# A GNN layer on one core: weights, bias and last nodes loaded by the Activation engine's queue

## The chip, the cores and the metric

One core of a Trainium2 chip runs the kernel. The metric is the device time of one execution in microseconds (us), lower being better. The kernel before was timed three times.

## The reference

With x of shape [5000, 64], a dense adjacency matrix adj of shape [5000, 5000] and everything in float32:

```python
h = jnp.maximum(_layernorm(x, axis=-1), 0.0)
neighbors = (adj @ h) / (num_neighbors[:, None] + 1e-7)
out = jnp.concatenate([h, neighbors], axis=-1) @ fc_w.T + fc_b   # fc_w is [64, 128]
return x + jax.nn.relu(out)
```

adj is 100 MB, everything else together under 3 MB.

## The kernel before, in words

The kernel uses that adj @ h @ W equals adj @ (h @ W). It first forms g = h @ W_neighbor for all nodes (64 columns), keeps it in SBUF as `g_sb`, and then multiplies adjacency tiles by it. So adj is read once, and every tile of it is used by TensorE as soon as g of its 128 source nodes is there.

**Loads of adj.** The host lays adj out transposed, in six groups of columns. A load (`LOADS`) is up to four row tiles of a group: in group 0 a load is 4 x 2560 floats for each of 128 lanes, one run of 40 KB a lane, 5,242,880 bytes. All 33 loads are issued by SP (line 259) in order into the buffer `raw`. In group 0 three loads fit in it. The fourth and later ones wait for `load_used`, which TensorE raises when it has multiplied the load whose place is taken (lines 255 to 256, 633 to 634). `landed` says that a load has arrived.

**Preparation.** The 40 row tiles of x are normalized in five sets of eight, b = 0 to 4. DVE and ACT compute the layer norm of a set (`normalize`, lines 407 to 436, `ln_square`, `ln_std`), TensorE transposes it (`turn`, line 579), ACT copies it to `ht` (line 357), TensorE multiplies it by the weights `w_both` (`weigh`, lines 582 to 598), and ACT copies the neighbour part to `g_sb` (line 363) while DVE adds the bias to the node's own part (`add_bias`, line 448). Set 0 comes before the first adjacency tile, sets 1 to 4 are put between tiles (`TURN_AFTER`, `WEIGH_AFTER`). Sets 0 to 3 need only the two main loads of x (`load_x`, semaphore `x_loaded[0]`). Set 4 also needs the last 392 nodes (`x_loaded[1]`), loaded in two pieces: lanes 0 to 95 (98,304 bytes) and lanes 96 and 97 (2 KB), the second only after DVE has cleared what pads them.

**Small loads.** The weights `fc_t` are loaded twice into `w_both`, in each load 64 lanes with two runs of 256 bytes, after DVE has cleared `w_both` (`weights_cleared`). The bias is one run of 256 bytes. A matrix product of ones and the bias row (line 683) spreads it over all lanes, and DVE copies it (`bias_copied`). It uses an accumulator that group 1 needs later. The 5000 neighbour counts `nn` are loaded by ACT (lines 331 and 333) after set 1 is transposed, the last 8 rows of adj by GpSimd (lines 294 to 299).

**Order on the queues before.** SP issues `load_x(0)`, `load_x(1)`, the 96 lanes of the last nodes (line 268), waits for `weights_cleared`, issues the weights twice (line 272), then adj. ACT runs one Sqrt first, which brings its table in (line 373), then issues the bias (line 325) and the two lanes (line 327). TensorE waits for the bias first, spreads it, then `turn(0)`, waits for the weights, `weigh(0)`, and starts on the loads.

Of the kernel before, what the change touches and what calls it, by code (L numbers as in the profile page):

```python
# [44 lines left out]
def gnn_layer(nc, x, adj_groups, num_neighbors, fc_t, fc_b, out):  # L45
# [9 lines left out]
    N, F = x.shape  # L55
# [11 lines left out]
    PAD0 = LAST_LANES // 32 * 32  # L67
# [56 lines left out]
    with ExitStack() as ctx:  # L124
# [8 lines left out]
        x_sb = sb("x_sb", [LANES, TILES, F])  # L133
# [13 lines left out]
        w_both = sb("w_both", [2 * F, 2, 2 * F])  # L147
# [65 lines left out]
        def tail(v):  # L213

            return v[0:LAST_LANES, ROWS:TILES, :].rearrange("p t f -> p (t f)")

        def tail_nodes(v):
            return v[TAIL0:N, :].rearrange("(p t) f -> p (t f)", t=RUN)
# [32 lines left out]
        def sync_program(sp):  # L251
            def load(n):
                g, m, i0, i1 = LOADS[n]
                w = WIDTH[g]
                if loads_before(n):
                    sp.wait_ge(load_used, loads_before(n))
                r = RUN if m < FULL else TAIL_RUN
                rows = adj_groups[g][m * BLOCK:m * BLOCK + r * LANES, 0:w].rearrange("(p i) c -> p (i c)", i=r)
                sp.dma_start(raw[:, place(n):place_end(n)], rows[:, i0 * w:i1 * w]).then_inc(loaded(n)[0], 16)

            def load_x(k):
                r = slice(ROWS // 2 * k, ROWS // 2 * (k + 1))
                sp.dma_start(x_sb[:, r, :], x[0:TAIL0, :].rearrange("(p r) f -> p r f", r=ROWS)[:, r, :]  # L263
                             ).then_inc(x_loaded[0], 16)

            load_x(0)
            load_x(1)
            sp.dma_start(tail(x_sb)[0:PAD0], tail_nodes(x)[0:PAD0]).then_inc(x_loaded[1], 16)  # L268
            sp.wait_ge(weights_cleared, 1)
            for s in range(2):  # L270
                k = slice(s * F, (s + 1) * F)
                sp.dma_start(w_both[k, s, :].rearrange("r (k c) -> r k c", k=2), fc_t.rearrange("(k r) c -> r k c", k=2)  # L272
                             ).then_inc(weights_loaded, 16)
            for n in range(len(LOADS)):
                load(n)

            sp.wait_ge(out_ready, LAST)
            sp.dma_start(out[0:TAIL0, :].rearrange("(p r) f -> p (r f)", r=ROWS), flat(out_sb[:, 0:ROWS, :])
                         ).then_inc(stored, 16)
            sp.wait_ge(stored, 16)  # L280
# [40 lines left out]
        def scalar_program(act):  # L321
            def load_few():

                act.wait_ge(bias_cleared, 1)
                act.dma_start(bias_row[0:1, :], fc_b.rearrange("(a f) -> a f", a=1)).then_inc(bias_loaded, 16)
                act.wait_ge(x_cleared, 1)
                act.dma_start(tail(x_sb)[PAD0:LAST_LANES], tail_nodes(x)[PAD0:LAST_LANES]).then_inc(x_loaded[1], 16)

            def load_counts():
                act.wait_ge(nn_cleared, 1)  # L330
                act.dma_start(nn[:, 0:ROWS], num_neighbors[0:TAIL0].rearrange("(p r) -> p r", r=ROWS)
                              ).then_inc(nn_loaded, 16)
                act.dma_start(nn[0:LAST_LANES, ROWS:TILES],
                              num_neighbors[TAIL0:N].rearrange("(p t) -> p t", t=RUN)).then_inc(nn_loaded, 16)

            def ln_square(b):
                act.wait_ge(ln_dve, LN_OPS * b + 3)
                nc.scalar.activation(sums[0][:], cen[:], ACT.Square).then_inc(ln_act, 1)  # L338

            def ln_std(b):  # L340
                act.wait_ge(ln_dve, LN_OPS * b + 5)
                nc.scalar.activation(std[:], var[:], ACT.Sqrt).then_inc(ln_act, 1)

            def copy_turned(b):
                act.wait_ge(turned_done, b + 1)
                if b >= 2:
                    act.wait_ge(weighed, b - 1)
                if b == SETS - 1:
                    act.wait_ge(rem_cleared, 2)

                    k = turned[HALF:LANES, :].rearrange("k (t p) -> k p t", t=RUN)[:, 0:LAST_LANES, :]
                    nc.scalar.activation(ht_rows[HALF:LANES, :].rearrange("k (p t) -> k p t", t=RUN), k, ACT.Copy)

                    nc.scalar.activation(
                        ht_rem[HALF:LANES, 0:REM * REM_STEP].rearrange("k (p t z) -> k p t z", t=RUN, z=REM_STEP)[:, :, :, 0],
                        k[:, LAST_LANES - REM // RUN:LAST_LANES, :], ACT.Copy)
                nc.scalar.activation(ht[b % 2][:], turned[:], ACT.Copy).then_inc(turned_copied, 1)  # L357

            def copy_g(b):
                act.wait_ge(weighed, b + 1)  # L360
                to = g_sb[:, BT * b:BT * (b + 1), :].rearrange("p (s i) f -> p i s f", s=2)
                for k in range(2):
                    nc.scalar.activation(to[:, 2 * k:2 * k + 2, :, :], weighed_parts(k, 1), ACT.Copy).then_inc(g_copied, 1)  # L363

            def copy_spread(b):
                act.wait_ge(spread_done, b + 1)
                w = BLOCK if b != ALONE else BLOCK // 2 + SIDE
                nc.scalar.activation(rnn_bc[:, b, 0:w], y[b % 2][:, 0:w], ACT.Copy).then_inc(spread_copied, 1)  # L368


            act.wait_ge(warm_ready, 1)
            nc.scalar.activation(std[:, 0:1], warm[:], ACT.Sqrt)
            load_few()
            for b in range(SETS):
                ln_square(b)
                ln_std(b)
                if b == 0:
                    copy_turned(0)
                else:
                    copy_g(b - 1)  # L380
                    copy_turned(b)
                if b == 1:
                    load_counts()
            copy_g(SETS - 1)
            for b in range(SETS):
                copy_spread(b)
            act.wait_ge(out_ready, LAST + 1)
            act.dma_start(tail_nodes(out), tail(out_sb)).then_inc(last_stored, 16)
            act.wait_ge(last_stored, 16)

        def vector_program(dve):
            nc.vector.memset(warm[:], 1.0).then_inc(warm_ready, 1)
            nc.vector.memset(x_sb[PAD0:LANES, ROWS:TILES, :], 0.0).then_inc(x_cleared, 1)
            nc.vector.memset(w_both[:], 0.0).then_inc(weights_cleared, 1)
            nc.vector.memset(nn[:], 1.0).then_inc(nn_cleared, 1)

            def parts(b):
# [174 lines left out]
        def tensor_program(pe):  # L572
            def turn(b):
                pe.wait_ge(ln_dve, LN_OPS * (b + 1))
                if b:
                    pe.wait_ge(turned_copied, b)
                for i in range(RUN):
                    c = slice(i * LANES, (i + 1) * LANES)
                    last = nc.tensor.transpose(turned[:, c], h_pairs[b % 2][:, c], ident[:])  # L579
                last.then_inc(turned_done, 1)  # L580

            def weigh(b):

                pe.wait_ge(turned_copied, b + 1)
                if b:
                    pe.wait_ge(self_copied, 2 * b)
                apart = b == SETS - 1
                w = 3 * F if apart else 4 * F
                for i in range(RUN):
                    c = i * LANES  # L590
                    last = nc.tensor.matmul(weighed_tiles(i)[:, 0:w], ht[b % 2][:, c:c + LANES], flat(w_both[:])[:, 0:w],  # L591
                                            start=True, stop=True)
                    if apart:

                        h = ht_rows[F:LANES, i:REM0 - TAIL0:TAIL_RUN] if i < TAIL_RUN else ht_rem[F:LANES, :]
                        last = nc.tensor.matmul(weighed_tiles(i)[:, w:4 * F], h, w_both[F:LANES, 1, F:2 * F],  # L596
                                                start=True, stop=True)
                last.then_inc(weighed, 1)
# [75 lines left out]
            def flip_last():  # L674
                for i in range(2):
                    pe.wait_ge(scaled, LAST + i + 1)
                    nc.tensor.transpose(acc[i][0:LAST_LANES, 0:2 * F], sums[0][:, i * LAST_LANES:(i + 1) * LAST_LANES],  # L677
                                        ident[:]).then_inc(flipped, 1)


            pe.wait_ge(bias_loaded, 16)
            pe.wait_ge(bias_cleared, 2)
            nc.tensor.matmul(acc[SETS - 1][:, 0:F], ones[:], bias_row[:], start=True, stop=True).then_inc(bias_spread, 1)  # L683
            pe.wait_ge(ident_ready, 1)
            turn(0)
            pe.wait_ge(weights_loaded, 32)
            weigh(0)
            for n in range(len(LOADS)):
                g, m, i0, i1 = LOADS[n]
                pe.wait_ge(*loaded(n))  # L690
# [55 lines left out]
```

## Time and profile before

| What | Value |
|---|---|
| median of 3 runs | 246.09 us (246.04 to 246.28) |
| the profiled execution | 245.87 us, its span 244.4 us |
| TensorE busy | 209.6 us, 86% of the span |
| VectorE, ScalarE, GpSimd busy | 41.6, 15.1, 6.1 us |
| DMA | 102.79 MB, mean 421 GB/s |
| mean granted TensorE clock | 0.965 |

The span goes from the first instruction to the last. The profiled execution took 1.5 us more than its span, and was 0.22 us below the median. Times within the span are counted from its start. In the slice table each digit is the busy share, in tenths, of one fortieth of the span, 6.1 us. PE is TensorE, DVE VectorE, ACT ScalarE, POOL GpSimd, SP SyncE. A name with q behind it is the engine's queue of issued DMAs.

### The profile page before, as it was taken

The page shows a single profiled execution, that of the slowest core. Times are in us where ns is not written, and L with a number is a line of the kernel's source. Part 1 is how long each engine was busy: PE and PEld are TensorE (multiplying, and loading weights), DVE is VectorE, ACT ScalarE, POOL GpSimd, SP SyncE. Part 2 cuts the span into 40 slices and gives each one's busy share as a digit, 9 for nine tenths or more (in the row PEclk, how much of TensorE's full clock was granted, in tenths as well). Part 3 has the DMA queues.
Part 4 walks back from the last instruction along what each step waited for, and adds up shares of the span by engine and source line. Part 5 has one row for each costly group of instructions (what it writes and reads, how often), then busy time and mean ns, then how long its engine had stood idle before and what let it go on. Part 6 is the DMA issues. An engine that isn't in the chain of part 4 may idle for free.

```text
span 244.4 us, 2432 instructions
## 1 busy us (share of the span) xinstructions
PE 209.6 (86%) x1086; PEld 87.2 (36%) x1086; DVE 41.6 (17%) x102; ACT 15.1 (6%) x34; POOL 6.1 (2%) x17
## 2 busy tenths in 40 slices
PE   0268999697869987999999898969999689997995
PEld 0143344242323532353334243414444224332354
DVE  1752033304400200023000530202100000000052
ACT  2130011101200110010000300000000000000000
POOL 6000020000000000000010000000000000000000
PEclk9999999999979997989999999979999979999999
DMA  8999999999999999999999999999999999999996
GB/s 321 429 429 429 429 428 415 430 429 442 426 429 429 436 425 429 429 429 411 410 456 422 447 431 441 415 415 463 434 415 415 456 429 400 429 429 412 416 395 268
DMA packets 6127, 102.79 MB, mean 421 GB/s; under 512 B 1266, under 2 KB 1854, under 8 KB 3046
## 3 DMA queue, kind: packets, MB, share of 16 engines
q1 hardware_dynamic: 5584, 102.37, 98.2%
q8 instruction: 8, 0.13, 0.2%
q10 hardware_dynamic: 374, 0.12, 0.2%
q0 software_dynamic: 160, 0.16, 0.2%
q14 instruction: 1, 0.01, 0.0%
HBM read 101.37 MB, written 1.28 MB: 420 GB/s over the span
## 4 chain that ended last, share of the span: by engine, by line
DMA 57%; PE 40%; SPq 1%; DVE 0%; issue 0%
DMA raw<-adj_group 57%; PE acc L631 33%; PE turned L631 4%; PE acc L646 1%; PE y L591 1%; PE y L596 1%; SPq L272 1%; PE y L659 0%; PE y L661 0%; SPq L263 0%; PE turned L579 0%; DVE out_sb L540 0%; SPq L268 0%; PE acc L677 0%; DVE sums L523 0%
## 5 line engine op out<-in xcount | busy, mean ns | idle before, releaser
L631 PE MATMUL acc<-raw,g_sb 128*64 128x512 f32 (+1 forms) x780 | 168.1, 579 | 20.1 <-DMA raw<-adj_group 20.1
L631 PEld LDWEIGHTS acc<-raw,g_sb 128*64 128x64 f32 x780 | 56.5, 142 | 112.3 <-issue 80.0
L631 PE MATMUL turned<-raw,g_sb 128*64 128x196 f32 x156 | 18.5, 342 | 0.1
L631 PEld LDWEIGHTS turned<-raw,g_sb 128*64 128x64 f32 x156 | 11.6, 140 | 15.9 <-issue 14.9
L448 DVE TENSOR_TENSOR out_sb<-y,bias 128x128 f32<-128x128 f32 x20 | 4.4, 283 | 55.0 <-ACT g_sb L363 55.0
L506 DVE TENSOR_TENSOR sums<-acc,rnn_bc 128x512 f32<-128x512 f32 x4 | 2.7, 688 | 63.3 <-PE acc L631 61.3
L591 PE MATMUL y<-w_both,ht 128*128 128x256 f32 (+1 forms) x40 | 12.1, 441 | 0.8 <-ACT ht L357 0.8
L591 PEld LDWEIGHTS y<-w_both,ht 128*128 128x128 f32 x40 | 8.0, 217 | 3.9 <-issue 2.7
L532 DVE TENSOR_TENSOR out_sb<-y,out_sb 128x512 f32<-128x512 f32 (+1 forms) x5 | 3.2, 636 | 25.8 <-PE y L659 21.9
L579 PE MATMUL turned<-ident,h_pairs 128*128 128x128 f32 x20 | 3.7, 315 | 4.0 <-DVE h_pairs L436 4.0
L424 DVE TENSOR_REDUCE var<-sums 128x8 f32<-128x512 f32 x5 | 3.4, 686 | 21.5 <-ACT sums L338 21.5
L363 ACT ACTIVATE g_sb<-y 128x256 f32<-128x256 f32 x10 | 3.3, 381 | 54.9 <-PE y L591 34.9
L683 PE MATMUL acc<-bias_row,ones 128*128 128x64 f32 x2 | 0.7, 450 | 6.6 <-DMA bias_row<-fc_b 6.6
L477 DVE TENSOR_TENSOR rnn_diag<-ident,rnn 128x512 f32<-128x512 f32 x8 | 5.1, 686 | 0.2 <-PE y L616 0.2
L616 PE MATMUL y<-rnn_diag,ones 128*64 128x512 f32 (+1 forms) x20 | 4.6, 552 | 0.5 <-DVE rnn_diag L477 0.4
L368 ACT ACTIVATE rnn_bc<-y 128x512 f32<-128x512 f32 (+1 forms) x5 | 2.9, 587 | 30.4 <-PE y L616 30.4
L482 DVE TENSOR_TENSOR rnn_diag<-ident_twice,rnn 128x256 f32<-128x256 f32 x1 | 0.4, 426 | 24.4 <-issue 24.4
L357 ACT ACTIVATE ht<-turned 128x512 f32<-128x512 f32 x5 | 3.0, 597 | 25.5 <-PE turned L579 25.5
L579 PEld LDWEIGHTS turned<-ident,h_pairs 128*128 128x128 f32 x20 | 2.4, 156 | 5.7 <-issue 5.7
L413 DVE TENSOR_REDUCE mean<-x_sb 128x8 f32<-128x512 f32 (+1 forms) x6 | 3.4, 588 | 4.6 <-DMA x_sb<-x 4.6
L646 PE MATMUL acc<-adj_rem,g_sb 128*64 128x512 f32 (+1 forms) x20 | 4.2, 549 | 0.0
L420 DVE TENSOR_TENSOR cen<-x_sb,mean 128x512 f32<-128x512 f32 (+1 forms) x6 | 3.5, 602 | 0.2
(60 smaller groups left out, 46.0 us busy)
## 6 DMA issues: line engine op xcount, KB each, us to landing
raw<-adj_group SPq DMA_DIRECT2D x9, 5120.0 KB, 27.0
raw<-adj_group SPq DMA_DIRECT2D x6, 4880.0 KB, 23.2
raw<-adj_group SPq DMA_DIRECT2D x4, 2048.0 KB, 20.6
raw<-adj_group SPq DMA_DIRECT2D x1, 4096.0 KB, 23.9
raw<-adj_group SPq DMA_DIRECT2D x1, 3840.0 KB, 22.8
raw<-adj_group SPq DMA_DIRECT2D x2, 1024.0 KB, 22.2
raw<-adj_group SPq DMA_DIRECT2D x4, 392.0 KB, 22.6
x_sb<-x SPq DMA_DIRECT2D x2, 576.0 KB, 4.4
```

What stands on the lines that cost most here:

```text
L363: nc.scalar.activation(to[:, 2 * k:2 * k + 2, :, :], weighed_parts(k, 1), ACT.Copy).then_inc(g_copied, 1)
L413: last = nc.vector.tensor_reduce(narrow(mean[:]), rows, AX_X, ALU.add)
L420: last = nc.vector.tensor_tensor(wide(cen[:]), rows, m.unsqueeze(len(m.shape)).to_broadcast(list(rows.shape)), ALU.subtract)
L424: nc.vector.tensor_reduce(var[:], sums[0][:].rearrange("p (t f) -> p t f", f=F), AX_X, ALU.add).then_inc(ln_dve, 1)
L448: last = nc.vector.tensor_tensor(to[:, 2 * k:2 * k + 2, :], weighed_parts(k, 0)[:, :, s, :], bias[:].unsqueeze(1).to_broadcast([LANES, 2, ...
L477: last = nc.vector.tensor_tensor(split(to[:, s, :]), ident[:].unsqueeze(1).to_broadcast(shape), rnn[:, m + s:ROWS:FULL].unsqueeze(2).to_br ...
L532: nc.vector.tensor_tensor(o, split(y[b % 2][:, 0:RUN * F * (m1 - m0)]), o, ALU.add).then_inc(summed, 1)
L579: last = nc.tensor.transpose(turned[:, c], h_pairs[b % 2][:, c], ident[:])
L591: last = nc.tensor.matmul(weighed_tiles(i)[:, 0:w], ht[b % 2][:, c:c + LANES], flat(w_both[:])[:, 0:w], start=True, stop=True)
L616: last = nc.tensor.matmul(y[b % 2][k, c], ones[:, 0:HALF], r, start=True, stop=True, tile_position=(0, s * HALF))
L631: last = nc.tensor.matmul(acc[b][s * HALF:(s + 1) * HALF, 0:width], g_sb[:, t, :], k, start=t == 0, stop=t == CH - 1, tile_position=(0, s ...
L646: last = nc.tensor.matmul(acc[b][s * HALF:(s + 1) * HALF, 0:width], g_sb[:, CH, :], k, start=False, stop=False, tile_position=(0, s * HALF))
```

## The change

The two weight loads and the 96-lane piece of the last nodes move from SP's queue to ACT's. ACT issues, as its first work and ahead of the Sqrt: weights, weights, bias, 96 lanes, 2 lanes. On SP's queue the first adjacency load follows x directly. DVE clears `w_both` first. TensorE spreads the bias behind `weigh(0)`.

```diff
             load_x(0)
             load_x(1)
-            sp.dma_start(tail(x_sb)[0:PAD0], tail_nodes(x)[0:PAD0]).then_inc(x_loaded[1], 16)
-            sp.wait_ge(weights_cleared, 1)
-            for s in range(2):
-                k = slice(s * F, (s + 1) * F)
-                sp.dma_start(w_both[k, s, :].rearrange("r (k c) -> r k c", k=2), fc_t.rearrange("(k r) c -> r k c", k=2)
-                             ).then_inc(weights_loaded, 16)
             for n in range(len(LOADS)):
                 load(n)
...
             def load_few():
+                act.wait_ge(weights_cleared, 1)
+                for s in range(2):
+                    k = slice(s * F, (s + 1) * F)
+                    act.dma_start(w_both[k, s, :].rearrange("r (k c) -> r k c", k=2),
+                                  fc_t.rearrange("(k r) c -> r k c", k=2)).then_inc(weights_loaded, 16)
                 act.wait_ge(bias_cleared, 1)
                 act.dma_start(bias_row[0:1, :], fc_b.rearrange("(a f) -> a f", a=1)).then_inc(bias_loaded, 16)
+                act.dma_start(tail(x_sb)[0:PAD0], tail_nodes(x)[0:PAD0]).then_inc(x_loaded[1], 16)
                 act.wait_ge(x_cleared, 1)
                 act.dma_start(tail(x_sb)[PAD0:LAST_LANES], tail_nodes(x)[PAD0:LAST_LANES]).then_inc(x_loaded[1], 16)
...
+            load_few()
 
             act.wait_ge(warm_ready, 1)
             nc.scalar.activation(std[:, 0:1], warm[:], ACT.Sqrt)
-            load_few()
...
         def vector_program(dve):
+            nc.vector.memset(w_both[:], 0.0).then_inc(weights_cleared, 1)
             nc.vector.memset(warm[:], 1.0).then_inc(warm_ready, 1)
             nc.vector.memset(x_sb[PAD0:LANES, ROWS:TILES, :], 0.0).then_inc(x_cleared, 1)
-            nc.vector.memset(w_both[:], 0.0).then_inc(weights_cleared, 1)
             nc.vector.memset(nn[:], 1.0).then_inc(nn_cleared, 1)
...
-            pe.wait_ge(bias_loaded, 16)
-            pe.wait_ge(bias_cleared, 2)
-            nc.tensor.matmul(acc[SETS - 1][:, 0:F], ones[:], bias_row[:], start=True, stop=True).then_inc(bias_spread, 1)
             pe.wait_ge(ident_ready, 1)
             turn(0)
             pe.wait_ge(weights_loaded, 32)
             weigh(0)
+
+            pe.wait_ge(bias_loaded, 16)
+            pe.wait_ge(bias_cleared, 2)
+            nc.tensor.matmul(acc[SETS - 1][:, 0:F], ones[:], bias_row[:], start=True, stop=True).then_inc(bias_spread, 1)
             for n in range(len(LOADS)):
```

## Rows read from the trace of the kernel before

**Rows 1.** The page: 40 slices of TensorE, of DMA and its rate.

```profile
PE   0268999697869987999999898969999689997995
DMA  8999999999999999999999999999999999999996
GB/s 321 429 429 429 429 428 415 430 429 442 426 429 429 436 425 429 429 429 411 410 456 422 447 431 441 415 415 463 434 415 415 456 429 400 429 429 412 416 395 268
```

**Rows 2.** The page: DMA queues, with packets, MB, share of the 16 engines.

```profile
q1 hardware_dynamic: 5584, 102.37, 98.2%
...
q10 hardware_dynamic: 374, 0.12, 0.2%
```

**Rows 3.** The chain of waits in order of time, to 57 us: start, length, what.

```profile
0.76 0.37 SPq L263
...
1.18 0.42 SPq L263
...
1.65 0.42 SPq L268
...
2.12 0.69 SPq L272
...
2.85 0.60 SPq L272
...
3.49 15.48 DMA raw<-adj_group
...
29.50 27.30 DMA raw<-adj_group
```

**Rows 4.** Stretches: us, busy of PE, PEld, DVE, ACT, POOL, clock, DMA share, GB/s.

```profile
1.70:2.20 0.50, 0.00 (x0) 0.00 (x0) 0.00 (x0) 0.49 (x2) 0.50 (x2) 1.00 0.80 129
2.20:2.80 0.60, 0.00 (x0) 0.00 (x0) 0.00 (x0) 0.04 (x1) 0.60 (x1) 1.00 0.72 200
2.80:5.00 2.20, 0.00 (x0) 0.00 (x0) 0.00 (x0) 0.00 (x0) 1.70 (x5) 1.00 1.02 419
...
18.00:30.10 12.10, 11.03 (x52) 4.10 (x52) 1.77 (x5) 0.02 (x1) 0.00 (x0) 1.00 1.00 430
```

**Rows 5.** Timeline to 20 us: start, length, instruction, idle before it.

```profile
0.82 0.06 DVE L392 MEMSET warm<- 128x1 f32 x1 [0.82 <-PEq L739]
...
1.38 0.27 DVE L394 MEMSET w_both<- 128x256 f32 x1
...
1.60 0.52 ACTq L325 DMA_DIRECT2D bias_row<-fc_b  x1
...
6.58 0.69 PE L683 MATMUL acc<-bias_row,ones 128*128 128x64 f32 x2 [6.58 <-DMA bias_row<-fc_b]
...
13.15 3.75 PE L591 MATMUL y<-w_both,ht 128*128 128x256 f32 x8 [0.78 <-ACT ht L357]
...
16.94 0.66 ACT L363 ACTIVATE g_sb<-y 128x256 f32<-128x256 f32 x2 [2.25 <-PE y L591]
...
19.02 7.43 PE L631 MATMUL acc<-raw,g_sb 128*64 128x512 f32 x30 [2.12 <-DMA raw<-adj_group]
```

**Rows 6.** DMA issues by line: count, KB each, us from issue to landing.

```profile
x_sb<-x SPq DMA_DIRECT2D x2, 576.0 KB, 4.4
...
w_both<-fc_t SPq DMA_DIRECT2D x2, 32.0 KB, 4.4
...
adj_rem<-adj_group POOLq DMA_DIRECT2D x1, 16.0 KB, 11.9
```

**Rows 7.** TensorE's timeline from 31 us, where it waited for a load.

```profile
31.14 4.52 PE L631 MATMUL acc<-raw,g_sb 128*64 128x512 f32 x24 [1.10 <-DMA raw<-adj_group]
...
44.63 8.81 PE L631 MATMUL acc<-raw,g_sb 128*64 128x512 f32 x48 [2.01 <-DMA raw<-adj_group]
...
56.84 4.52 PE L631 MATMUL acc<-raw,g_sb 128*64 128x512 f32 x24 [1.48 <-DMA raw<-adj_group]
...
69.09 10.51 PE L631 MATMUL acc<-raw,g_sb 128*64 128x512 f32 x48 [2.70 <-DMA raw<-adj_group]
```

**Rows 8.** Who waited for whom, whole span: us in total, times, longest.

```profile
PE acc L631 <- DMA raw<-adj_group: 20.1, 12, 3.0
```

**Rows 9.** The end of TensorE's timeline, from 235 us.

```profile
235.24 1.61 PE L631 MATMUL turned<-raw,g_sb 128*64 128x196 f32 x16
...
237.37 4.05 PE L631 MATMUL turned<-raw,g_sb 128*64 128x196 f32 x44
```

## The prediction

> **What bounds the kernel now.** I read the slice table first. The DMA engines are busy to nine tenths and more from the second slice to the last but one, at about 429 GB/s, while TensorE has slices of 6 and 7 [rows 1]. Of the engines' time 98.2% goes to SP's queue q1 alone [rows 2], which carries x and adj. So the span is the time at which adj's first byte moves, plus 101 MB at a nearly fixed rate, plus a tail. TensorE waits for adjacency loads 20.1 us in all, 2.1 of it before the first one [rows 5, 8]: it is second in line, with some 18 us of room over the whole run. After the last such wait it has its own tail [rows 9], which moves with the landings.
>
> The chain of waits seems to say something else: at its start stand SP's issues one behind the other, x, the last nodes, the weights twice, and adj only at 3.49 us [rows 3]. Without the last nodes and the weights the first adjacency load would be issued at 1.65, 1.84 us earlier. But an issue is not a transfer. The stretches show when the DMA engines themselves work: they start at about 1.7 us, are filling up until 2.8, and from 2.8 on are full (share 1.02, 419 GB/s) [rows 4]. x, last nodes and weights are 1,179,648 + 100,352 + 65,536 bytes, 1.35 MB. From 1.7 to 2.8 some 0.18 MB moved, the other 1.17 MB at 419 GB/s need 2.8 us, so they end at about 5.6 us. adj issued at 3.49 is ready about 1.0 us later (x: issue 0.76, first bytes 1.7), at 4.5, before its turn. No engine stood idle for want of adj.
>
> **The change part by part.**
>
> (1) SP's three issues removed, 1.84 us [rows 3]. What hides them is x's own transfer. Gain: nothing by itself. Between 1.7 and 2.8 the engines moved 0.18 MB where 0.46 could have gone, so 0.28 MB or 0.65 us of room is there. Weights issued by ACT at 1.13 could use a little of it: the 64 KB are 0.15 us. Bounds: 0 to 0.15 us gained with certain reasons, and 1.84 us if my reading of the start were wrong. I take 0.1.
>
> (2) The same bytes on ACT's queue. They are still moved by the same 16 engines, so adj begins earlier by what it later gives back. The Trainium skill, page "DMA: Bandwidth & Descriptors", section "Issuing engines are not separate DMA queues", says that issuing from several engines saves only the sequencers' time; by it the sum stays as in (1).
>
> (3) DVE clears w_both first: 0.82 + 0.27 = 1.09 us [rows 5]. ACT then issues weights at 1.13 and 1.8, bias at 2.45, 96 lanes at 3.0, two lanes at 3.4, each 0.25 to 0.69 long as before, then the Sqrt with its table, 1.5 us, ending near 5.3. ACT is first wanted at 7.9. Nothing. The nn loads that ACT issues later keep their place behind these in its queue.
>
> (4) The bias product goes behind weigh(0): 0.7 us on TensorE that now stand before the first load instead of at 6.6 [rows 5]. TensorE has 2.1 us of waiting there, so nothing, unless the weights are late.
>
> (5) When do the weights land? That is the real question, since TensorE takes the first load only behind weigh(0). Before, they were 4.4 us in flight and landed at 7.3 [rows 3, 6], 5.8 us before they were wanted. Now they share each DMA engine with adj. q10 had 374 packets: nn 128 + 98, out 98, bias 1, two lanes 2, together 327 runs, and a rest of 47 completions (16, 14, 14, 1, 2). So each run is a packet of its own [rows 2]. The weights are 2 x (128 + 16) = 288 packets, 18 on each engine. An adjacency packet in group 0 is 40,960 bytes, and 16 of them at 430 GB/s take 1.52 us [rows 4]. If the queues take turns packet by packet, a weight packet costs 1.52 us beside adj, but only 0.18 us beside x (4,608 bytes). That turns happen is to be seen in a small load issued by GpSimd amid adj: 16 KB needed 11.9 us [rows 6]. And the bias, 256 bytes issued at 1.60 while x flowed, was there only at 6.58 [rows 5]: a latecomer waits for what the engine has already taken in, 3 us and more.
>
> Here a rule would give another sum. The Trainium skill, page "DMA: Bandwidth & Descriptors", section "Queues, rings and completion order", has an engine drain a whole packet, typically 9 to 17 descriptors, before it changes the queue. By it each weight load is one packet an engine, two turns, 3 us. The 374 packets of q10 say otherwise and I go by them.
>
> Bounds for the weights' landing: all beside x, about 6 us; all 18 beside adj, from 5.2 us on, 17 steps of which two fall on borders between adjacency loads, where q1's own packet is only a completion: 5.2 + 15 x 1.52 + 0.5 = 28.5 us; with a first turn two packets late, 31.5. I take the middle: the first weight load is ready at 2.1 us, ahead of adj's 2.65, and its runs get in behind x; its completion and the nine packets of the second, ready at 2.8, do not. That is ten turns, one on a border: 5.2 + 9 x 1.52 + 0.5 = 19.4 us. weigh(0) 3.75, the bias 0.7 [rows 5] (its two packets come meanwhile): the first load is multiplied from 23.8 instead of 19.0, TensorE is 4.8 us late.
>
> What does lateness cost? The fourth load is issued when the first is used up, at 29.50 [rows 3]. Three loads from 5.4 at 430 GB/s end at 42.0. With 1.0 us to get going the engines run dry only when the issue is later than 41.0: **11.5 us of cover**. Less than that costs nothing, as TensorE catches up in its waits, 1.10 + 2.01 + 1.48 + 2.70 us up to 69 us [rows 7]. The later loads' issues have as much or more room, since TensorE is no longer later by then. The 96 lanes follow at seven turns and more, by 40 to 50 us, and set 4 wants them after 55. nn, some 17 turns behind, comes before it is needed near 65 to 70.
>
> Sum: 245.87 - 0.1 for the profiled execution, that is 246.0 for the median, which is 0.22 above it.
>
> **The rivals.** A measurement of this kernel tells a difference from about 0.2%, 0.49 us.
>
> *A. The weights starve, slower (0.39).* Both loads fall behind adj. Weights 28.5, first load from 32.9, TensorE 13.9 us late, against a cover of 11.5. The fourth load is issued at 43.4, the engines stand dry for 2.4 us, and as they are the bound this stays to the end: 248.4. A first turn two packets later gives 251.4. For it: bias and the 16 KB load waited as said; the second weight load is ready after adj. Against it: the first is ready before adj. It decides from the point where more than about 15 of the 18 packets fall beside adj.
>
> *B. The issue time was the bound, faster (0.09).* Then adj flows up to 1.84 us sooner: 244.2. The full share from 2.8 us speaks against it. A part of it, 0.6 us, could come if the small runs cost the engines more in front of adj than between its packets, 245.4.
>
> *C. Nothing moves (0.12).* All weights get in beside x, or whole loads in one turn as the skill's rule has it. The first load begins at 19 to 20 us: 246.0 as well, but without lateness of TensorE.
>
> **How the numbers follow.** The forecast with half of the weights late has 0.40, C 0.12: same 0.52; A 0.39; B 0.09. Range: below to 245.5, which takes in the small part of B; above to 249.8, all of A but the late first turn. The likeliest case's own range is 245.7 to 246.4.
>
> **What would show it.** Right: first adjacency issue at 1.65, weights issued from 1.13, DMA full from 2.8 as before; TensorE's first row of line 591 begins between 17 and 22 us after a wait for w_both, its first wait for adj disappears, the waits of rows 7 shrink one after the other, and landings from the fourth load on stand where they stood. A shows line 591 at 28 us and a fourth adjacency issue later than 41 us, with a slice of lower DMA share near 43. C shows line 591 at 13. B shows the second load's landing 0.5 us or more before 31.1. Wrong altogether would be a first landing of adj unlike 18.5 to 19.

## The result: slower, and spread over six microseconds

| Kernel | Median of 22 runs | Lowest to highest |
|---|---|---|
| before | 246.19 us | 245.93 to 246.58 |
| changed | 248.57 us | 246.23 to 252.09 |

The ratio of the two medians over all runs is 248.57 / 246.19 = 1.0097. The ratio given with an interval, 1.0061 (1.0044 to 1.0077), leaves out the six runs more than 1.5% above the fastest, though their granted clocks (0.986 to 1.000) are like the others' and e4 below shows that lateness alone gives such times. The profiled execution took 247.26 us and its span was 245.8 us, both 1.4 us more than in the profile of before. None of the 22 executions but this one has a trace.

The slice table of the changed kernel (TensorE, DMA, its rate) against [rows 1], and its queues against [rows 2]:

```profile
PE   0100699999999998998599999979899689997995
DMA  8999999899999999999999999999999999999996
GB/s 304 429 429 428 414 434 433 342 429 414 440 417 427 433 433 429 447 453 413 423 447 415 430 419 473 413 419 428 464 419 413 448 427 405 427 427 415 412 394 259
...
q1 hardware_dynamic: 5184, 102.20, 97.9%
q10 hardware_dynamic: 774, 0.29, 0.5%
```

TensorE stands still in slices 3 and 4, from 12 to 24 us, and has then hardly a gap until 90 us. DMA has a dent in the eighth slice, 43 to 49 us: 8 for 9, 342 GB/s for 430. 400 packets have moved from q1 to q10. That is 2 x 144 of the weights and 96 + 16 of the last nodes, so a run has a packet of its own, as counted before.

The chain of waits to 31 us, which starts with the weights and no longer with adj [rows 3]:

```profile
0.87 0.28 DVE w_both L393
...
1.18 0.68 ACTq L322
...
1.89 24.16 DMA w_both<-fc_t
...
26.09 3.79 PE y L592 x8
...
29.91 0.67 ACT g_sb L364 x2
...
30.71 10.86 PE acc L632 x48
```

Each row has start, length and what. The second weight load, 32 KB, was 24.2 us in flight where it had been 4.4 [rows 6]. SP's and TensorE's timelines around the fourth adjacency load:

```profile
1.66 1.77 SPq L259 DMA_DIRECT2D raw<-adj_group  x3
...
41.60 0.33 SPq L259 DMA_DIRECT2D raw<-adj_group  x1
```

```profile
26.09 3.78 PE L592 MATMUL y<-w_both,ht 128*128 128x256 f32 x8 [13.58 <-DMA w_both<-fc_t]
...
42.09 4.52 PE L632 MATMUL acc<-raw,g_sb 128*64 128x512 f32 x24
...
53.49 8.81 PE L632 MATMUL acc<-raw,g_sb 128*64 128x512 f32 x48
```

The first adjacency load is issued 1.8 us earlier, as the diff makes it, but takes 17.3 us to land: it is there at 18.9 us, and was at 19.0 before [rows 3].

```profile
raw<-adj_group SPq DMA_DIRECT2D x1, 5120.0 KB, 17.3
```

The fourth is issued at 41.60 instead of 29.50, when the three loads in the ring have about run out. The waits of [rows 7] at 31, 44 and 56 us are gone, because TensorE is now the later one.

### The profile page after: what moved, and what is told of

Read it like the earlier page. It is cut to its first block, busy times and chain, and to the rows that moved or that the text cites. A ratio compares the mean times of both kernels' runs of the same rounds, so it can differ in the third digit from the quotient of the medians.

```text
span 245.8 us, 2432 instructions
## 1 busy us (share of the span) xinstructions
PE 204.5 (83%) x1086; PEld 88.2 (36%) x1086; DVE 41.7 (17%) x102; ACT 15.1 (6%) x34; POOL 6.1 (2%) x17
## 4 chain that ended last, share of the span: by engine, by line
DMA 49%; PE 49%; DVE 0%; issue 0%; ACTq 0%; ACT 0%
DMA raw<-adj_group 39%; PE acc L632 38%; DMA w_both<-fc_t 10%; PE y L592 4%; PE turned L632 4%; PE turned L580 1%; PE acc L647 1%; PE y L660 0%; PE y L662 0%; ACTq L322 0%; ACT g_sb L364 0%; DVE out_sb L541 0%; PE acc L678 0%; DVE w_both L393 0%; DVE sums L524 0%
## 5 line engine op out<-in xcount | busy, mean ns | idle before, releaser
L632 PE MATMUL acc<-raw,g_sb 128*64 128x512 f32 (+1 forms) x780 | 163.8, 567 | 12.9 <-DMA raw<-adj_group 12.4
L592 PE MATMUL y<-w_both,ht 128*128 128x256 f32 (+1 forms) x40 | 12.1, 442 | 13.6 <-DMA w_both<-fc_t 13.6
L433 DVE TENSOR_TENSOR cen<-cen,rstd 128x512 f32<-128x512 f32 x5 | 3.5, 692 | 0.2
(60 smaller groups left out, 43.4 us busy)
## 6 DMA issues: line engine op xcount, KB each, us to landing
raw<-adj_group SPq DMA_DIRECT2D x1, 4096.0 KB, 24.2
```

The costliest lines, as they stand in the source:

```text
L433: nc.vector.tensor_tensor(c, c, bcast(rstd[:]), ALU.mult).then_inc(ln_dve, 1)
L632: last = nc.tensor.matmul(acc[b][s * HALF:(s + 1) * HALF, 0:width], g_sb[:, t, :], k, start=t == 0, stop=t == CH - 1, tile_position=(0, s ...
```

## The experiments

Theory L (lateness) says: packets of the weights take turns with 40 KB packets of adj, TensorE starts late, and once the fourth adjacency issue comes after about 41 us, the DMA engines run dry (have nothing left to move) and the end moves by that much. The rivals are other parts of the change (R1), SP's issue time (R2), a late service of ACT's queue whatever stands beside it (R3), engines slowed by the turns themselves (R4), and bytes instead of packets as what sets the landing (R5). Each experiment is compared with runs of the kernel before that were taken beside it; their medians lie between 246.14 and 246.26 us.

**e1: the weights back on SP's queue**, behind x and before adj, and taken out of `load_few`.

```diff
+            sp.wait_ge(weights_cleared, 1)
+            for s in range(2):
+                k = slice(s * F, (s + 1) * F)
+                sp.dma_start(w_both[k, s, :].rearrange("r (k c) -> r k c", k=2), fc_t.rearrange("(k r) c -> r k c", k=2)
+                             ).then_inc(weights_loaded, 16)
             for n in range(len(LOADS)):
                 load(n)
```

> The changed kernel with the two weight loads put back on SP's queue, between x and adj; the last nodes stay on ACT's queue and the bias product behind weigh(0). Theory L (lateness: the weights' packets take turns with 40 KB adjacency packets on each DMA engine, TensorE starts late, and past about 11 us of lateness the three-load ring runs empty): weights land near 7.3 us, the first adjacency product is at 19 us, the time is 246.2 like before and hardly spreads. Rival R1 (the other moves, bias product or last nodes, cost): 247 or more and a spread of some us as in the changed kernel. Rival R2 (SP's issue time counts): 0.5 us or more above a kernel that issues adj at 1.65.

Measured: 246.28 us (246.01 to 246.47), ratio 1.0002 (0.9993 to 1.0011). In its profile the weights landed at 7.3 us and the first adjacency product began at 19.34. The last nodes on ACT's queue and the bias product behind weigh(0) cost nothing, and the spread is gone. R1 falls.

**e2: adj issued later, the weights where the change put them.** SP first waits until GpSimd has cleared two buffers, at about 4.06 us.

```diff
+            sp.wait_ge(rem_cleared, 2)
             for n in range(len(LOADS)):
                 load(n)
```

> The changed kernel, with SP waiting for GpSimd's clearing of adj_rem and ht_rem (about 4.06 us) before it issues the first adjacency load; the weights stay on ACT's queue. adj is then ready at about 5.1 us, when x ends between 5.0 and 5.6. Theory L, with the race between weights and adj as the cause: all weight packets are taken in before adj, weights land by 6 to 8 us, first product 19 us, time 246.0 to 246.4, no spread. Rival R3 (ACT's queue is served late whatever stands on SP's): weights still land past 15 us, time 247 to 250. Rival R2 (issue time counts): 2.4 us later issue gives 2 us more than the changed kernel.

Measured: 246.24 us (246.02 to 246.30), ratio 0.9999 (0.9991 to 1.0008). The timeline of this kernel:

```profile
1.18 1.34 ACTq L323 DMA_DIRECT2D w_both<-fc_t  x2
...
4.09 1.28 SPq L259 DMA_DIRECT2D raw<-adj_group  x3
...
13.39 3.75 PE L593 MATMUL y<-w_both,ht 128*128 128x256 f32 x8 [0.78 <-ACT ht L359]
...
19.49 7.03 PE L633 MATMUL acc<-raw,g_sb 128*64 128x512 f32 x20 [2.02 <-DMA raw<-adj_group]
```

adj is issued 2.4 us later than in the changed kernel, and all is well: weigh(0) waits only for ACT's copy. So ACT's queue is not late in itself (R3 falls), it is late when adj is there first. And the time of the first adjacency issue, 3.49 before and 4.09 here, is worth nothing; e3 below has it at 1.65 and is at 246.08 (R2 falls).

**e3 and e4: lateness without turns.** The weights are taken out of `load_few` and stand on SP's queue behind the first or the second adjacency load, so order alone makes them late. The diff is e3's, e4 has `n == 1`.

```diff
             for n in range(len(LOADS)):
                 load(n)
+                if n == 0:
+                    sp.wait_ge(weights_cleared, 1)
+                    for s in range(2):
+                        k = slice(s * F, (s + 1) * F)
+                        sp.dma_start(w_both[k, s, :].rearrange("r (k c) -> r k c", k=2), fc_t.rearrange("(k r) c -> r k c", k=2)
+                                     ).then_inc(weights_loaded, 16)
```

> As e1, but the weight loads stand on SP's queue behind the first adjacency load, so in one queue and with no turns: they land at about 18.6 us by order alone. weigh(0) from 18.7, first product at 23.4, TensorE 4.4 us late. Theory L: within the cover, 246.2. Rival R4 (small packets taking turns with large ones slow the engines themselves, and TensorE's lateness is harmless): 246.2 too. If any lateness of TensorE costs its own length: 250.5.

> As e3, but behind the second adjacency load: weights land at about 30.8 us, first product at 35.5, TensorE 16.5 us late, still with no turns taken between queues. Theory L: fourth adjacency issue at about 46.3, engines dry for about 5 us, time 250.5 to 251.5, little spread. Rival R4 (turns slow the engines, lateness harmless): 246.2.

Measured: e3 246.08 us (245.91 to 246.48), ratio 0.9997 (0.9987 to 1.0006); e4 251.72 us (250.45 to 252.48), ratio 1.0216 (1.0189 to 1.0243). TensorE in e3, then in e4, where SP's last row spans the third adjacency issue and the fourth, which ends at 45.57:

```profile
19.51 3.78 PE L593 MATMUL y<-w_both,ht 128*128 128x256 f32 x8 [7.37 <-DMA w_both<-fc_t]
...
24.13 8.81 PE L633 MATMUL acc<-raw,g_sb 128*64 128x512 f32 x48 [0.52 <-ACT g_sb L365]
```

```profile
31.77 3.78 PE L593 MATMUL y<-w_both,ht 128*128 128x256 f32 x8 [19.34 <-DMA w_both<-fc_t]
...
36.39 8.82 PE L633 MATMUL acc<-raw,g_sb 128*64 128x512 f32 x48 [0.52 <-ACT g_sb L365]
...
4.29 41.28 SPq L259 DMA_DIRECT2D raw<-adj_group  x2
```

```profile
42.00:44.00 2.00, 2.00 (x14) 0.92 (x12) 0.00 (x0) 0.00 (x0) 0.00 (x0) 1.00 0.00 0
```

5 us of lateness cost nothing, 17 us cost over 5, and the last row (e4's stretch from 42 to 44 us; the last two numbers are DMA share and GB/s) shows the engines moving nothing. R4 falls: the weights took no turns here (bias and last nodes, on ACT's queue still, did so in e1 too, at no cost). The four times of e4 reach above the expected 250.5 to 251.5, and that they spread by 2 us was not expected.

**e5: half the packets.** The second weight load is left out, so the odd tiles' products with the weights are missing from the result.

```diff
-                for s in range(2):
+                for s in range(1):
...
-            pe.wait_ge(weights_loaded, 32)
+            pe.wait_ge(weights_loaded, 16)
```

> The changed kernel with only the first of the two weight loads (s = 0); the half of w_both that the second one fills stays zero, so the odd tiles' products with the weights are left out of the result, while all instructions on the engines stay. 9 packets on each DMA engine instead of 18. In the profile of the changed kernel the weights landed at 26.0 us, some 14 turns of 1.52 us after 5.2, so about 4 packets had got in before adj. Theory L: 9 minus 4, 5 turns, landing near 13 us (at most 5.2 + 8 x 1.52 + 0.5 = 18 us), TensorE at most 4 us late, time 246.2, no spread. Rival R3 (ACT's queue is served late whatever it holds, by a delay and not by turns): landing again past 22 us, time 247 to 250.

Measured: 246.27 us (246.02 to 246.49), ratio 1.0004 (0.9994 to 1.0014).

```profile
17.34 3.78 PE L592 MATMUL y<-w_both,ht 128*128 128x256 f32 x8 [4.93 <-DMA w_both<-fc_t]
```

The weights landed at 17.3, near the upper bound of 18 and not at 13: on the slowest of the engines nearly all packets of this load took a turn (17.3 is 7.6 turns behind 5.7). The time is as expected, and R3, which wanted a landing past 22 us, falls here too.

**e6: twice the packets for the same bytes.**

```diff
-                    act.dma_start(w_both[k, s, :].rearrange("r (k c) -> r k c", k=2),
-                                  fc_t.rearrange("(k r) c -> r k c", k=2)).then_inc(weights_loaded, 16)
+                    for h in range(0, F, F // 2):
+                        act.dma_start(w_both[k, s, :].rearrange("r (k c) -> r k c", k=2)[:, :, h:h + F // 2],
+                                      fc_t.rearrange("(k r) c -> r k c", k=2)[:, :, h:h + F // 2]
+                                      ).then_inc(weights_loaded, 16)
...
-            pe.wait_ge(weights_loaded, 32)
+            pe.wait_ge(weights_loaded, 64)
```

> The changed kernel with each weight load cut in two loads of half the columns: the same bytes in runs of 128 bytes, 36 packets on each engine instead of 18. Theory L: turns go on until SP's three loads are through at about 42 us and the engines stand empty; then all that is left of the weights goes at once. Weights land at 42 to 43 us, first product near 47, fourth adjacency issue near 57, engines dry for 15 us: time 260 to 262, and less spread than the changed kernel. Rival R5 (bytes, not packets, set the landing): 247 to 250 as the changed kernel.

Measured: 262.74 us (262.29 to 263.07), ratio 1.067 (1.0653 to 1.0687).

```profile
44.27 3.78 PE L594 MATMUL y<-w_both,ht 128*128 128x256 f32 x8 [32.01 <-DMA w_both<-fc_t]
...
57.74 0.33 SPq L259 DMA_DIRECT2D raw<-adj_group  x1
```

```profile
44.00:57.00 13.00, 12.21 (x54) 7.05 (x56) 2.56 (x8) 0.66 (x2) 0.00 (x0) 1.00 0.00 0
```

With the same 64 KB cut in runs of 128 bytes the kernel is 16.5 us above the one before, where it was 2.4 above with runs of 256. They landed only when adj had run out, and then no engine moved a byte for 13 us (the second fence is that stretch). Packets decide, not bytes (R5 falls). The time was 0.7 us above the expected 260 to 262.

**e7: short turns.** Only the first adjacency load is cut, in four of one row tile, with runs of 10 KB.

```diff
-STEPS = [ALL, ALL, LESS, LESS, LESS, LESS]
+STEPS = [(1, *ALL[1:]), ALL, LESS, LESS, LESS, LESS]
```

> The changed kernel with the first adjacency load of group 0 cut in four loads of one row tile: runs of 10 KB instead of 40 KB, a turn of 0.38 us instead of 1.52 while the first 5 MB go by. Everything of the change stays. Theory L: 14 to 17 turns of 0.38 us, less one at each border, weights land at 10 to 12 us, first product at or before 19 us, time 246.0 to 246.3, no spread. Rival R3: landing and time as in the changed kernel.

Measured: 246.64 us (246.22 to 247.00), ratio 1.0018 (1.0009 to 1.0027).

```profile
1.65 3.29 SPq L259 DMA_DIRECT2D raw<-adj_group  x6
...
13.22 3.75 PE L592 MATMUL y<-w_both,ht 128*128 128x256 f32 x8 [0.78 <-ACT ht L358]
...
31.97 6.02 PE L632 MATMUL acc<-raw,g_sb 128*64 128x512 f32 x24 [3.00 <-DMA raw<-adj_group]
```

The weights landed at 11.5 us, within the expected 10 to 12, although nothing of the change was taken back, and the large spread is gone: the length of a turn is the cost. But 0.4 us remain, just outside the expected 246.0 to 246.3. TensorE has the load after the cut ones at 31.97 here and at 31.14 before [rows 7].

**e11: the same cut in the kernel before**, to see whose the 0.4 us are.

> The kernel before with its first adjacency load cut in four loads of one row tile, as in e7 (246.64 us there, 0.4 above before, though the weights were in time). If the shorter runs of 10 KB or the three more loads cost that by themselves, this one is at 246.5 to 246.8 too; if it was what is left of the turns between the queues, it is at 246.2.

Measured: 246.38 us (246.15 to 246.71), ratio 1.0007 (0.9998 to 1.0016). It lies between the two answers. TensorE has the load after the cut ones at 31.74 here, so most of its delay comes with the cut and not with the turns. Whether the 0.4 us of time do stays open.

**e8 and e9: the changed kernel twice more**, for the landing beside the time.

> The changed kernel once more, one look, for the landing of the weights beside its time. Theory L: the time above 246.2 is the fourth adjacency issue's time above about 40.5 us (41.6 gave 247.3); the landing is at 5.7 us plus a whole number of 1.52 us turns. Any time between 246.2 and 252 is allowed, but not a time above 248 with a landing before 26, nor 246.2 with a landing after 27.

> As e8, one more look at the changed kernel: the pair of landing and time must lie on the same line, time = 246.2 + (fourth adjacency issue - 40.5) and never below 246.2.

| Kernel | weights landed | first product | 4th adj issue | time of that run | 246.2 + (issue - 41.0) |
|---|---|---|---|---|---|
| before | in time | 19.02 | 29.50 | 245.87 | below the limit |
| e3 | 19.5 | 24.13 | 32.98 | 245.91 | below the limit |
| changed | 26.1 | 30.71 | 41.60 | 247.26 | 246.8 |
| e9 | 27.3 | 31.96 | 43.16 | 248.90 | 248.4 |
| e8 | 29.5 | 34.19 | 43.54 | 248.83 | 248.7 |
| e4 | 31.7 | 36.39 | 45.24 | 250.45 | 250.4 |
| e6 | 44.2 | 48.89 | 57.74 | 263.07 | 262.9 |

In these rows "4th adj issue" is when SP issues the fourth adjacency load, which is as soon as TensorE has used up the first. From e4 to e6 the issue moves by 12.5 us and the time by 12.6, one for one. Carried down from e4, the line meets 246.2 at an issue time of 41.0. My expectation for e8 and e9 had 40.5 from the first profile alone, which gives 249.2 and 248.9. Measured were 248.83 and 248.90: 41.0 is nearer for e8, 40.5 for e9, and either value leaves all five late profiles within about half a microsecond. So the edge is known to half a microsecond and no better. The landing as a whole number of turns did not hold: 29.5 and 27.3 are 15.7 and 14.2 turns behind 5.7.

**e10: an attempt at a gain.** ACT issues the second half of x while SP issues the first, the weights are back on SP.

```diff
             load_x(0)
-            load_x(1)
+            sp.wait_ge(weights_cleared, 1)
+            for s in range(2):
+                k = slice(s * F, (s + 1) * F)
+                sp.dma_start(w_both[k, s, :].rearrange("r (k c) -> r k c", k=2), fc_t.rearrange("(k r) c -> r k c", k=2)
+                             ).then_inc(weights_loaded, 16)
...
             def load_few():
+                r = slice(ROWS // 2, ROWS)
+                act.dma_start(x_sb[:, r, :], x[0:TAIL0, :].rearrange("(p r) f -> p r f", r=ROWS)[:, r, :]
+                              ).then_inc(x_loaded[0], 16)
```

> An attempt to gain from the start: the second half of x is issued by ACT at the same moment as SP issues the first, SP then issues the weights and adj, ACT the bias and the last nodes. x's two halves take turns with each other, and the weights stand before adj in one queue. If the room between 1.7 and 2.8 us (0.65 us, in which the DMA engines fill up) is due to late descriptors, the time is 245.7 to 246.0; if it is the latency of the first reads, 246.2 as before. Theory L expects weights at 7 us and no spread.

Measured: 246.22 us (245.90 to 246.61), ratio 0.9999 (0.9990 to 1.0008). x was issued from both queues at 0.75 us, and still only 0.13 MB moved between 1.7 and 2.8 us (83 and 154 GB/s in the two stretches of [rows 4], which had 0.18 MB): issuing x sooner does not fill that time. No version here beats the kernel before.

## Why the prediction was wrong in its number and right in its mechanism

**Bound and part (1), right.** The transfer, not the issue, sets the start: issued 1.8 us earlier, the first adjacency load landed within 0.1 us of when it did, and e3, with the same early issue, is at 246.08. e2 shows it from the other side: an adjacency issue 2.4 us later changes nothing. Rival B is out.

**Parts (2) to (4), right.** e1 has the last nodes and the bias product as changed, and is at 246.28.

**The price of a turn, right.** One packet each, 1.52 us beside 40 KB: e5, e6 and e7 change the number of turns and their length, and the landing follows. The 374 packets of q10 alone did not show this, since they say how runs are recorded and not when an engine changes the queue; the landings do. By the rule of the Trainium skill, page "DMA: Bandwidth & Descriptors", section "Queues, rings and completion order", a whole weight load, nine runs and completions on each engine, could have gone in one turn. The trace does not agree: the second landed at 26.1 us and not near 8.

**The cover, right to about half a microsecond.** I had the engines run dry for issues later than 41.0; the line of e4 and e6 gives 41.0, that of the changed kernel's first profile 40.5. Only the step from the first product to the fourth issue was taken as fixed, at 10.5 us, and it is not: it was 8.8 to 11.2 us (last section).

**The step that failed is the weights' landing in part (5)**: the middle value, "the first weight load is ready at 2.1 us, ahead of adj's 2.65, and its runs get in behind x". It had the weights land at 19.4. In the profile of the changed kernel the first load landed at 13.6 (1.18 + 12.4) and the second at 26.1. Measured from 5.7, that is 13.4 turns where I counted 9 steps. I reasoned for one average engine, but a load has landed when the slowest of 16 is through. The trace's packet records show it: of 257 runs of 256 bytes, weights and bias, 119 moved between 5 and 6 us, nearly half, as I thought for the average; yet the last one moved at 24.0, and its completion took one turn more. And I gave the landing one value for all executions: three profiles had 26.1, 27.3 and 29.5. That the few tenths of a microsecond between the first weight packets and the first adjacency packets decide it anew each time is my reading and was not tested. The number of weight and bias runs moved before 6 us, 119, 100 and 104 in the same order, does not give the order of the landings.

The median of 248.57 lies inside my range of 245.5 to 249.8, but it is not the forecast of 246.0 with no change: it is rival A's number, 248.4. The chain of rival A, which had first product 32.9, issue 43.4 and time 248.4, is what e8 and e9 show: 34.19 and 31.96, 43.54 and 43.16, 248.83 and 248.90. Of the 22 runs, six are at 246.2 to 246.9, near the forecast, and the other 16 from 247.26 up to 252.09, where A had 251.4 for a late first turn. No run of the six was profiled, so whether the weights were earlier there, or TensorE faster, is not known. The three profiles all had landings of 26.1 or later; none had the forecast's 19.4. Of the chances, 0.52 for no change was too much: A's own condition, "more than about 15 of the 18 packets beside adj", has only to hold on one engine of 16. By my own sum the changed kernel's landing at 26.1 gives an issue at 41.0, just on the edge; it came at 41.60, mostly because the first load took 10.86 us and not 10.5.

## What to carry to other kernels

A small load with a deadline should not share the DMA engines with a stream of long packets from another queue: here it paid up to one long packet, 1.52 us, for each of its runs on the slowest engine. Put it ahead of the stream on the same queue, or hold the stream until it has been taken in; the issue time saved by spreading over queues was worth nothing here, where the engines were busy. A stage that starts late was free up to the depth of the ring ahead of it (about 11 us here) and cost one for one beyond, so work out that depth before moving anything. When a moved step races with another, ask for the spread and not only for one profile.

## What the runs showed of the hardware that was not expected

The 48 products of the first adjacency load took TensorE 8.8 us in e3 to e6, 9.3 in e8, 10.9 in the changed kernel's profile and 11.2 in e9. This is why e9, whose weights landed 2.2 us before e8's, was no faster. The traces show what makes the difference. These are products of one shape, with count, busy time and mean ns of one: the first eight of the changed kernel (30.7 to 34.1 us), the first eight of e4 (36.4 to 38.1), and four of the changed kernel between 121 and 122 us, with the row of that stretch, whose granted clock is 0.50:

```profile
L632 PE MATMUL acc<-raw,g_sb 128*64 128x512 f32 x8 | 3.7, 1071 | 0.5 <-ACT g_sb L364 0.5
...
L633 PE MATMUL acc<-raw,g_sb 128*64 128x512 f32 x8 | 1.9, 605 | 0.5 <-ACT g_sb L365 0.5
...
L632 PE MATMUL acc<-raw,g_sb 128*64 128x512 f32 x4 | 1.9, 1061 | 0.0
...
121.00:122.00 1.00, 1.00 (x4) 0.50 1.07 461
```

So in the changed kernel and e9 (whose first eight have the same mean, 1071 ns), and in e8 for the first two products, the load began at the pace that goes with a granted clock of 0.50, the lower of TensorE's two levels (1.2 GHz). The stretch rows give 1.00 there, but the trace's own clock records begin only at 34.87 us in the changed kernel, 36.76 in e9, 35.26 in e8 and 36.44 in e4, and the pace doubles at just these times. Ahead of weigh(0) TensorE had stood idle, from 12 us until the weights were there. What sets the moment at which the clock rises stays open. The record begins at 22.34 us in the kernel before, so there too the load took 10.4 us and not 8.8. The lateness thus has two parts, the landing and this. An estimate from these rows: at the full clock from 30.71 on, the changed kernel's fourth issue would have come at 39.5, inside the cover, and its profiled execution would have lost nothing.

And e4, in which order alone delays the weights, still spreads from 250.45 to 252.48, so not all spread needs the turns between queues. Its one profile, the fastest of its four runs, had the full clock for the whole first load. The up to 2.4 us that the lower clock cost elsewhere would cover the 2.0 us, but no other run of e4 has a trace, so this is not shown.
